# Counting the passed shifts inside the tridiagonalisation's last stage: the sign count moves from VectorE to GpSimd, one matmul moves up TensorE's queue, and the last blocks of the diagonal are cut smaller

## The reference, cut to what matters

```python
def _L0_gnn_ref(features, A, W1, b1, W2, b2):
    deg = jnp.sum(A, axis=0) + jnp.sum(A, axis=1) - jnp.diagonal(A)
    d_inv_sqrt = jnp.where(deg > 0, jax.lax.rsqrt(deg), 0.0)
    L = jnp.diag(deg) - A
    L_norm = d_inv_sqrt[:, None] * L * d_inv_sqrt[None, :]
    _, U = jnp.linalg.eigh(L_norm)
    agg = jnp.einsum('mn,bnd->bmd', U.T, features)
    h = jax.nn.relu(agg @ W1 + b1)
    out = h @ W2 + b2
    return jnp.einsum('nm,bmd->bnd', U, out)
```

## Time and profile before

| | |
|---|---|
| time, median of 3 runs | 1349.13 us (1346.92 to 1349.48) |
| the profiled execution: its own time | 1349.69 us |
| the profiled execution: span, first to last instruction | 1348.0 us |
| granted TensorE clock, mean | 0.928 |
| busy: PE / PEld / VectorE / ScalarE / GpSimd | 1068.0 / 881.1 / 987.8 / 807.0 / 308.2 us |
| VectorE stands before L418 (for GpSimd) | 8.01 us |
| VectorE stands before L630 (for TensorE's L550) | 24.75 us |
| TensorE stands before L553 (for VectorE's L694) | 45.96 us |

### The profile page before, as it was taken

The page is one execution under the profiler, slowest core; times in us unless marked ns, Lnnn a source line. Parts: engine busy times, 40 slices in busy tenths (PEclk is TensorE's granted clock), DMA queues, the critical chain, the costliest instruction groups (busy, mean ns, idle before and its releaser), DMA issues.

```text
span 1348.0 us, 23938 instructions
## 1 busy us (share of the span) xinstructions
PE 1068.0 (79%) x6223; PEld 881.1 (65%) x6223; DVE 987.8 (73%) x4612; ACT 807.0 (60%) x2953; POOL 308.2 (23%) x1149
## 2 busy tenths in 40 slices
PE   6887777777757640899887899887899887999785
PEld 4666666666646530679766679766689666689564
DVE  7888888888862999545678645679655779556777
ACT  4555555555533320477777677777677786677785
POOL 4444445454560000101110201110211111111201
PEclk9999999999998675899988999988999988999887
DMA  4000000000000540200000300000300000000001
GB/s 132 1 1 1 1 2 1 1 1 2 1 0 1 140 126 0 63 1 1 1 0 2 96 1 1 1 1 9 88 1 1 1 1 19 14 1 2 1 1 32
DMA packets 45237, 25.46 MB, mean 19 GB/s; under 512 B 1921, under 2 KB 44066, under 8 KB 45090
## 3 DMA queue, kind: packets, MB, share of 16 engines
q1 hardware_dynamic: 45090, 23.81, 6.2%
HBM read 15.42 MB, written 8.39 MB: 18 GB/s over the span
## 4 chain that ended last, share of the span: by engine, by line
PE 34%; DVE 12%; ACT 9%; issue 3%; POOL 1%; DVEq 0%; POOLq 0%; ACTq 0%
PE P L1181 12%; PE P L1129 6%; PE P L1189 6%; PE P L1134 2%; ACT x L1283 2%; ACT S L1351 2%; DVE stats L1390 2%; PE P L1243 2%; DVE S L1462 2%; DVE top L1467 1%; DVE t L1480 1%; PE P L1198 1%; PE P L1227 1%; POOL t L1117 1%; ACT t L1331 1%
## 5 line engine op out<-in xcount | busy, mean ns | idle before, releaser
L1110 POOL TENSOR_TENSOR rstd<-variance,minus_half 128x4 f32<-128x4 f32 x64 | 64.5, 1007 | 434.1 <-DVE variance L1400 434.1
L282 PE MATMUL productP<-M,ident_tail 128*128 128x127 f32 (+63 forms) x254 | 87.3, 441 | 61.2 <-DVE M L409 61.0
L1181 PE MATMUL P<-t,WihT 128*128 128x128 f32 (+1 forms) x832 | 119.4, 290 | 10.0 <-POOL t L1117 10.0
L1189 PE MATMUL P<-step_h,WhhT 128*128 128x128 f32 (+2 forms) x768 | 123.4, 304 | 0.0
L1303 ACT ACTIVATE gate_i<-P,half_bias 128x128 f32<-128x128 f32 (+3 forms) x160 | 69.1, 432 | 88.4 <-PE P L1189 65.3
L1181 PEld LDWEIGHTS P<-t,WihT 128*128 128x128 f32 x832 | 109.9, 191 | 13.6 <-POOL t L1117 12.9
L282 PEld LDWEIGHTS productP<-M,ident_tail 128*128 128x128 f32 x254 | 63.7, 311 | 81.9 <-DVE M L409 81.9
L1189 PEld LDWEIGHTS P<-step_h,WhhT 128*128 128x128 f32 x768 | 108.9, 191 | 4.5 <-DVE step_h L1433 0.7
L277 PE MATMUL tailP<-ident_tail 128*128 128x128 f32 (+63 forms) x254 | 87.7, 443 | 19.7 <-DVE ident_tail L393 8.6
L1420 DVE SCALAR_TENSOR_TENSOR gate_i<-gate_i,gate_g 128x128 f32<-128x128 f32 (+2 forms) x96 | 38.6, 402 | 84.2 <-ACT gate_g L1303 84.2
L1351 ACT ACTIVATE S<-S,ntop 128x128 f32<-128x128 f32 x256 | 98.6, 391 | 0.0
(11 more groups left out here) (331 smaller groups left out, 3043.6 us busy)
## 6 DMA issues: line engine op xcount, KB each, us to landing
x_here<-x SPq DMA_DIRECT2D x16, 256.0 KB, 3.0
xin<-x SPq DMA_DIRECT2D x16, 256.0 KB, 2.9
feature_products<-made SPq DMA_DIRECT2D x16, 256.0 KB, 2.4
xw<-feature_products SPq DMA_DIRECT2D x16, 256.0 KB, 3.2
out<-y SPq DMA_DIRECT2D x16, 256.0 KB, 2.3
W<-L_gnn_W SPq DMA_DIRECT2D x3, 64.0 KB
Wqkv<-L_gnn_W SPq DMA_DIRECT2D x1, 192.0 KB
Wg<-L_gnn_Wg SPq DMA_DIRECT2D x2, 64.0 KB
```

The lines of the kernel that those rows point to most:

```text
L282: pe.matmul(productP[:, remaining], tails, M[:, remaining], start=True, stop=True).then_inc(product_ready, 1)
L1110: nc.gpsimd.tensor_tensor(rstd[s][:], variance[s][:], minus_half[:], ALU.pow).then_inc(S_("rstd_ready"), 1)
L1181: last = pe.matmul(place, c["WihT"][:, p - 1, gate * H:(gate + 1) * H], sources(s, p, t), start=bank not in fresh, stop=not t, skip_group_ ...
L1189: last = pe.matmul(gate_place(s, p, t, gate), c["WhhT"][:, p - 1, gate * H:(gate + 1) * H], step_h[s][:, 0:G * windows(p)], start=False, s ...
```

## The change

- GpSimd no longer keeps all polynomials but three of them in turn (`minor`). After each step it counts the sign itself (`count_sign`): product of two neighbouring minors, "greater than 0", addition to `passed` [128, 16]; each of the three waits for the one before.
- VectorE's L620, L621 and L622 are gone; `a` is made from `passed`.
- TensorE's sum of `a` moves from behind `turn` into the basis, ahead of level 2, and goes to the bank `madeP` of the products; `multiply` waits on `passed_read` once.
- The blocks of the diagonal are cut at CUTS = 0, 4, ..., 124, 126, 128. The last two reflections take two steps of the recurrence each, so that four are left after the last reflection, not six. From m = 120 on nothing is rescaled, and the phase of the rescaling moves by one step.
- Behind `open_gain`, GpSimd's order is now: square the edges, count, rescale, take the diagonal.

```diff
+CUTS = list(range(0, N - BATCH + 1, BATCH)) + [N - 2, N]
@@
-    polynomials = sb("polynomials", [N, N + 1, SHIFTS])
+    polynomials = sb("polynomials", [N, 3, SHIFTS])
+    agree = sb("agree", [N, SHIFTS])
+    passed = sb("passed", [N, SHIFTS])
@@
+            def minor(i):
+                return polynomials[:, i % 3, :]
@@
+            def count_sign(m):
+
+                c.step(nc.gpsimd.tensor_tensor(agree[:], minor(m + 1), minor(m), ALU.mult))
+                c.step(nc.gpsimd.tensor_scalar(agree[:], agree[:], 0.0, None, ALU.is_gt))
+                last = nc.gpsimd.tensor_tensor(passed[:], passed[:], agree[:], ALU.add)
+                if m < N - 1:
+                    c.step(last)
+                else:
                     last.then_inc(coarse_ready, 1)
@@
+            def minors_of_step(k):
+                lag = CUTS[1] + 1
+                if k < REFLECTIONS - 2:
+                    return [k - lag] if k >= lag else []
+                first = REFLECTIONS - 2 - lag
+                return [first + 2 * (k - REFLECTIONS + 2), first + 2 * (k - REFLECTIONS + 2) + 1]
@@
-                if k > BATCH:
-                    next_polynomial(k - BATCH - 1)
+                for m in minors_of_step(k):
+                    next_minor(m)
                 pool.wait_ge(inverses_ready, now)
                 nc.gpsimd.tensor_tensor(open_gain[:], inverses[:, 1:2], below[:, now:now + 1],
                                         ALU.mult).then_inc(open_gain_ready, 1)
-                if now % BATCH == 0:
-                    take_diagonal(k // BATCH)
-                elif k > 0 and k % BATCH == 0:
-                    square_edges(k // BATCH - 1)
-                if k > BATCH:
-                    keep_size(k - BATCH - 1)
+                if k in CUTS[1:]:
+                    square_edges(CUTS.index(k) - 1)
+                for m in minors_of_step(k):
+                    count_sign(m)
+                    if m < N - 8:
+                        keep_size(m)
+                if now in CUTS:
+                    take_diagonal(CUTS.index(now) - 1)
@@
-            take_diagonal(N // BATCH - 1)
-            square_edges(N // BATCH - 1)
-            for m in range(REFLECTIONS - BATCH - 1, N):
-                next_polynomial(m)
-                if m < N - 1:
-                    keep_size(m)
+            for m in range(minors_of_step(REFLECTIONS - 1)[-1] + 1, N):
+                next_minor(m)
+                count_sign(m)
+                if m == N - 4:
+                    take_diagonal(len(CUTS) - 2)
+                    square_edges(len(CUTS) - 2)
@@ spectral_vectors, tensor
             for level in range(LEVELS):
+                if level == 2:
+                    pe.wait_ge(passed_ready, 1)
+                    pe.matmul(passedP[:, 0:1], a[:], ones[:, 0:1], start=True, stop=True).then_inc(passed_summed, 1)
@@
             turn(pe)
-
-            pe.wait_ge(passed_ready, 1)
-            pe.matmul(outP[:, 0:1], a[:], ones[:, 0:1], start=True, stop=True).then_inc(passed_summed, 1)
+            pe.wait_ge(passed_read, 1)
             multiply(pe)
@@ spectral_vectors, vector
-            t.step(V.tensor_tensor(q[:], polynomials[:, 1:N + 1, :], polynomials[:, 0:N, :], ALU.mult))
-            t.step(V.tensor_scalar(negative[:], q[:], 0.0, None, ALU.is_gt))
-            t.step(V.reduce_sum(count[:], negative[:].rearrange("p i s -> p s i"), AX_X))
```

More of the change, by code:

```diff
@@ L182, in _ @@
             g.done(nc.gpsimd.memset(half_power[:], -0.5))
+            g.done(nc.gpsimd.memset(passed[:], 0.0))
             g.step(nc.gpsimd.memset(polynomials[:, 0, :], 1.0))
@@ L205, in next_polynomial, with next_minor @@
+            def next_minor(m):
+                pool.wait_ge(diag_kept, 1 + max(b for b in range(len(CUTS)) if CUTS[b] <= m))
+                here = D[:, m:m + 1].to_broadcast([N, SHIFTS])
                 if m == 0:
-                    c.step(nc.gpsimd.tensor_tensor(new, grid[:], D[:, 0:1].to_broadcast([N, SHIFTS]), ALU.subtract))
+                    c.step(nc.gpsimd.tensor_tensor(minor(1), grid[:], here, ALU.subtract))
                     return
-                part = c.done(nc.gpsimd.tensor_tensor(weighted[:], grid[:], D[:, m:m + 1].to_broadcast([N, SHIFTS]), ALU.subtract))
@@ L209, in next_polynomial @@
-                c.done(nc.gpsimd.tensor_tensor(new, old, nE2[:, m - 1:m].to_broadcast([N, SHIFTS]), ALU.mult))
+                part = c.done(nc.gpsimd.tensor_tensor(weighted[:], grid[:], here, ALU.subtract))
+                c.done(nc.gpsimd.tensor_tensor(minor(m + 1), minor(m - 1), nE2[:, m - 1:m].to_broadcast([N, SHIFTS]), ALU.mult))
                 c.until(part)
-                c.step(nc.gpsimd.tensor_tensor(weighted[:], weighted[:], now, ALU.mult))
-                last = nc.gpsimd.tensor_tensor(new, new, weighted[:], ALU.add)
@@ L214, in next_polynomial @@
                     last.then_inc(coarse_ready, 1)
-                    return
-                c.step(last)
             def keep_size(m):
-                new, now = (polynomials[:, i, :] for i in (m + 1, m))
                 middle = slice(SHIFTS // 2, SHIFTS // 2 + 1)
-                if m % RESIZE == 4:
+                new, now = minor(m + 1), minor(m)
+                if m % RESIZE == 3:
                     c.step(nc.gpsimd.tensor_scalar(reach[:, 0:1], now[:, middle], now[:, middle], 1.0e-37, ALU.mult, ALU.add))
@@ L269, in spread_diagonal @@
                 pe.wait_ge(diag_masked, b + 1)
-                pe.matmul(diagP[:, 0:BATCH], ones[:], diagonal[b % 2][:], start=True, stop=True).then_inc(diag_ready, 1)
+                many = CUTS[b + 1] - CUTS[b]
+                pe.matmul(diagP[:, 0:many], ones[:], diagonal[b % 2][:, 0:many], start=True, stop=True).then_inc(diag_ready, 1)
             def reflect(k, remaining, parity):
@@ L277, in reflect @@
                 pe.matmul(tailP[:, now:N + 1], tails, ident_tail[:, now:N + 1], start=True, stop=True).then_inc(tail_row_ready, 1)
[L278 to L279 removed]
+                if k in CUTS[1:]:
+                    spread_diagonal(CUTS.index(k) - 1)
                 pe.wait_ge(matrix_ready, now)
@@ L1534, in program @@
             with ExitStack() as part:
-                E, D, nE2, polynomials = spectral_basis(nc, held, psum_of(part), sem, d["adj"], A, ident_tail, ones, reflectors, gains,
+                E, D, nE2, passed = spectral_basis(nc, held, psum_of(part), sem, d["adj"], A, ident_tail, ones, reflectors, gains,
                                       borders, (load, fetch, first_residuals))
```

54 lines of the change are left out of this document (28 added, 26 removed).

## The result

The changed kernel takes 1334.74 us (median of 4 runs, 1334.3 to 1337.21) against 1348.81 us (median of 4, 1346.92 to 1349.48). The ratio is 0.9902, with a 95% interval of 0.9885 to 0.9919: faster by 1.0%, inside the range, and 3.7 us slower than forecast. Profiled again later it took 1335.91 us (median of 4), a ratio of 0.9912 (0.9897 to 0.9927).

What follows compares the result with a forecast made beforehand. No full engine bounds the reflections, but a loop passing between engines; VectorE's chain from L630 bounds block 2. Terms -30.7 + 9.3 + 3.2 = -18.2 us against 1349.69 gave 1331 us, range 1325 to 1338.

Steps and rivals of the forecast that it cites:

- TensorE's queue place: Block 2: summing `a` ahead of level 2, not behind the turned weights, with VectorE's three instructions gone, gains 30.7 us.
- The meeting of `a`'s loop with `joins`: Block 2: VectorE's loop making `a` runs beside GpSimd's seven `joins` and is delayed 1.0 us, bounds 0 and 3.2.
- Overruns where squaring and reach meet: Reflections with k divisible by 8: GpSimd's work of 3.52 us exceeds the period, costing 8.0 us over 15 reflections.
- the term of 9.3 us for the reflections: Block 1: loss from GpSimd's overruns at k divisible by 8 and k = 4 modulo 8, 10.8 us less 1.5.
- The 1.5 us that I took off: Reflections: estimated deduction from 10.8 us of overruns, six meetings where an already longer period leaves the count room.
- The ordinary reflections, costed at nothing: Block 1: GpSimd's 2.12 us of work including the count fits the period of 2.78 to 3.06 us, costing nothing.
- The end of block 1: GpSimd's queue from `open_gain` of k = 124 to L418 takes 18.9 us instead of 15.8, a loss of 3.2.
- Block 3 unchanged: Behind `Yb`: block 3 keeps its length; a changed length would show the prediction wrong.
- A hidden count: First rival: the count hides everywhere in the reflections, only the end of block 1 grows, 1321 us; 6%.
- L393 held up in each reflection: Rival: GpSimd's counting delays VectorE's L393 in all 122 reflections with a count, 25.6 us more, 1356 us; 4%.
- the end of block 2: Rival: TensorE, not VectorE's chain, ends block 2; it would need to lose 15 us more; under 1%.
- the second, more overruns: Rival: reflections overrun more with the count at 1.0 us (5.6 us), or full lock-out adds 2.2; 1339 us; 10%.

Runs made afterwards that it cites:

- move_only: Kernel before with only TensorE's sum of `a` moved ahead of level 4 of the basis (bank `madeP`), VectorE still counting: 1325.12 us, ratio 0.9832.
- count_only: Changed kernel with TensorE's sum of `a` put back behind the turned weights, counting still on GpSimd: 1367.05 us, ratio 1.0141 to the kernel before.
- early_count: Matmul ahead of level 2, shorter end, all polynomials kept; VectorE counts 120 while waiting for GpSimd in block 1, the last 8 after: 1317.44 us, ratio 0.977.
- spread_resize: Changed kernel with only the rescaling put at other reflections, so none of it meets the squaring of the edges: 1325.59 us, ratio 0.9837 to before.
- blind_count: Changed kernel with each counting instruction replaced by a waited GpSimd memset of 128x144 that reads nothing: 1332.45 us (one run).

## Why the prediction was right, point by point

- **TensorE's queue place is the gain**: right. -30.95 us from the sign fix of E to `LO`, forecast -30.7. That the two agree so closely is luck: in the second pair of profiles it is 38.61 - 9.56 = 29.05 us. move_only and count_only show the parts: the matmul's place alone gives 23.8, the three removed instructions give their 7.6 only together with it.
- **The meeting of `a`'s loop with `joins`**: 0.65 us, taken as 1.0. By the locking for whole instructions it would have been 3.2. The Trainium skill (SBUF — State Buffer, Who interferes with whom) calls the shared port pair an exclusive lock and says that two SBUF inputs on VectorE contend with a GpSimd instruction that reads SBUF; that the other engine stands for the whole instruction it says only of another mode of VectorE, so the prediction read more into it. What GpSimd suffers fits even that reading: 2.13 us beside 2.16 in early_count. Where the instructions of both are short, both lose little: VectorE 0.65 us in the loop beside seven `joins`, the `joins` 0.05 us each (0.50 us in place of 0.45, medians of L541 and L516), and a reflection at most some 0.03 us.
- **Overruns where squaring and reach meet**: right in place and mechanism (spread_resize). For the fifteen reflections k = 8 to 120 it is 9.4 us against 8.0 (the 8.53 of the table and 0.84 behind k = 120). For k = 4 modulo 8 it is 3.0 against 2.8. A waited counting step was priced at 0.30 us; the comparison needs 0.33.
- **The step that failed** is the term of 9.3 us for the reflections: `open_gain` of k = 124 came 394.07 - 376.55 = 17.5 us later. Three things are in the 8.2 us of difference. The overruns themselves were 1.6 us larger (9.4 + 3.0 against 10.8). The 1.5 us that I took off for room in already long periods come on top: such room shows in one period alone (k = 73, 3.25 us long before, grew by 0.28 instead of 0.7), and the 9.4 hold it already. The ordinary reflections, costed at nothing, grew by 4.9 us up to k = 119 and by 0.2 behind it; with the count they fit into the period, but they are not free. blind_count bounds the reads' share of that by 2.7 us; the rest stays open.
- **The end of block 1**: 413.53 - 394.07 = 19.5 us against 18.9 added up, so +3.7 instead of +3.2. TensorE was held for the block of two as said (its `spread_diagonal` of k = 126 waited 0.86 us), and GpSimd was the later one.
- **Block 3 unchanged**: wrong in these runs. It is shorter by 5.5 us in the profile. The way from `Yb` to the first load of the next samples is 14.3 us before and 13.6 after: the granted clock is at 1.2 GHz there, until 10.7 us behind `Yb` before and 8.9 after. That covers 0.7 us. In the whole block the granted clock was at 1.2 GHz for 107 us before and for 92 after. The twelve profiles go the same way: 88 to 92 us at 1.2 GHz in the three of 801 us, 95 to 102 in the six of 804 to 806, 106 to 107 in the three of 806 to 807. What puts those spells where they are stays open.
- **Rivals.** A hidden count is out (block 1 +21.2, not +3.2). L393 held up in each reflection is out: the growth at it is not seen, and the ordinary periods grew by 0.05 us, not 0.21. TensorE was not the end of block 2 (20.62 and 13.57 us to spare, forecast about 15). In block 1 the closest is the second, more overruns, whose 18.1 us were passed; with block 3 as before the time would have been 1348.8 + 21.2 - 30.9 = 1339, a microsecond above my range. The first rival takes 31.4 us for block 2, for which the working gives no sum beyond the 30.7; no run here shows it.

## What to carry to other kernels

Before moving work to an engine with idle time, add up its queue in the worst period, not its mean load: GpSimd was busy for half of the reflections' time (184.34 of 384 us), and yet one reflection in eight became 0.6 us too long and another 0.2. A small instruction that waits in an in-order queue behind unrelated work can be worth more than the work that it closes; try its move alone, since here that beat the whole change (1325.12 against 1334.74 us). Work whose result is only needed later belongs in a wait that the same engine has anyway: that took the time from 1322.8 to 1317.4 us here.

## What the runs showed of the hardware that I had not expected

- In early_count GpSimd's 16-column instruction stood for VectorE's whole long one when that read two SBUF tensors (2.13 beside 2.16 us) or was a comparison from SBUF to SBUF (1.11 beside 1.16), and not for a sum over 1920 columns (0.21 beside 3.35 us).
- VectorE lost little to GpSimd's short instructions: sixteen VectorE instructions beside seven `joins` of 0.45 to 0.50 us (and GpSimd's mask of 0.68 us behind them) took 0.65 us longer in all. No run here sets a GpSimd instruction of several microseconds beside them.
- The same block 3 took between 801.2 and 807.0 us in twelve profiles, in step with the time that the granted clock spent at 1.2 GHz (88 to 107 us); a comparison of stages needs that in view before a few microseconds are put down to an edit.
